# First attention: another order of the projections, scores and transposes on TensorE

## What is computed

```python
x = x + jnp.tanh(g_xattn[0]) * _L0_xattn_ref(ctx_768, _layernorm(x, axis=-1), mask_BxS2_bk0, ...)
x = x + jnp.tanh(g_ffn[0]) * _L0_ffn_ref(_layernorm(x, axis=-1), ...)
...
x = x + jnp.tanh(g_xattn[3]) * _L3_xattn_ref(_layernorm(x, axis=-1), ctx_768, ...)
x = x + jnp.tanh(g_ffn[3]) * _L3_ffn_ref(_layernorm(x, axis=-1), ...)
```

## Time and profile before

| what | us |
|---|---|
| median of the three runs | 1800.82 |
| lowest, highest | 1793.05, 1805.83 |
| the profiled execution's own time | 1798.77 |
| its span, first to last instruction | 1796.9 |

### The profile page before, as it was taken

One profiled execution on the slowest core, in us unless ns is written; L12 is line 12 of the kernel. 1 busy time (PEld: TensorE's weight loads), 2 busy tenths in 40 slices (PEclk: granted clock), 3 DMA queues, 4 the chain that ended last, 5 costly groups with the idle time before them and its releaser, 6 DMA issues.

```text
span 1796.9 us, 31011 instructions
## 1 busy us (share of the span) xinstructions
PE 1619.2 (90%) x9150; PEld 1153.7 (64%) x9150; DVE 981.3 (55%) x3200; ACT 624.8 (35%) x1772; POOL 333.5 (19%) x465
## 2 busy tenths in 40 slices
PE   6898899859999999999999999799998998887787
PEld 2555555659999866666666667567776446665555
DVE  4778787542222244444444435645555666884764
ACT  3555555412323233333333333133332004552232
POOL 4555555320000130000000000100000122333000
PEclk8999999869999989999999989899998999998887
DMA  4000005248999610000000000100000001310000
GB/s 109 15 18 20 20 19 146 65 138 298 321 327 319 232 41 13 7 12 12 12 12 6 1 4 16 31 26 19 19 25 1 27 25 35 91 56 1 1 19 19
DMA packets 86297, 115.80 MB, mean 64 GB/s; under 512 B 16610, under 2 KB 77762, under 8 KB 81090
## 3 DMA queue, kind: packets, MB, share of 16 engines
q1 hardware_dynamic: 82722, 110.43, 19.1%
q0 software_dynamic: 2432, 4.34, 0.8%
q10 hardware_dynamic: 1056, 0.01, 0.0%
HBM read 104.51 MB, written 6.95 MB: 62 GB/s over the span
## 4 chain that ended last, share of the span: by engine, by line
PE 73%; issue 9%; DVE 7%; ACT 4%; DMA 2%; POOL 2%; ACTq 1%; SPq 0%; DVEq 0%; POOLq 0%
PE bank L2293 14%; PE bank L2406 8%; PE bank L2589 7%; PE bank L2379 5%; PE bank L2682 5%; PE bank L2352 5%; PE bank L2390 4%; PE bank L2436 4%; PE bank L2603 3%; PE bank L2344 3%; PE bank L2635 3%; PE bank L2651 3%; PE bank L2754 2%; DMA work<-in_F_b1c 2%; DVE work L1542 1%
## 5 line engine op out<-in xcount | busy, mean ns | idle before, releaser
L1052 ACT ACTIVATE work<-bank,work 100x361 f32<-100x361 f32 (+1 forms) x272 | 158.9, 591 | 253.5 <-DVE work L1542 231.6
L1551 DVE COPY work<-bank 128x300 f32<-128x300 f32 (+1 forms) x272 | 123.2, 490 | 175.6 <-PE bank L2390 174.9
L2406 PEld LDWEIGHTS bank<-work 128*100 128x100 f32 x1760 | 185.4, 171 | 45.5 <-issue 31.4
L2406 PE MATMUL bank<-work 128*100 128x64 f32 (+1 forms) x1760 | 188.2, 258 | 4.2 <-DVE work L1551 4.2
L2589 PE MATMUL bank<-work 128*128 128x128 f32 x1216 | 144.4, 277 | 3.7 <-DMA work<-in_F_b1c 3.7
L1905 DVE SCALAR_TENSOR_TENSOR work<-bank,work 128x128 f32<-128x128 f32 x160 | 56.1, 351 | 163.8 <-PE bank L2589 151.6
L2589 PEld LDWEIGHTS bank<-work 128*128 128x128 f32 x1216 | 142.0, 193 | 5.3 <-issue 3.5
L1542 DVE TENSOR_REDUCE work<-bank 100x1 f32<-100x361 f32 x208 | 101.8, 528 | 70.9 <-PE bank L2379 65.7
L823 POOL TENSOR_TENSOR work<-work,neg_half 100x1 f32<-100x1 f32 x96 | 52.5, 547 | 391.8 <-DVE work L1498 390.1
L2379 PE MATMUL bank<-work 64*100 64x361 f32 (+1 forms) x512 | 119.0, 542 | 1.1 <-ACT work L1037 0.6
L2293 PE MATMUL bank<-L_WkvT,work 96*128 96x512 f32 x192 | 98.2, 637 | 15.8 <-ACT work L1013 14.9
(11 more groups left out here) (306 smaller groups left out, 2907.9 us busy)
## 6 DMA issues: line engine op xcount, KB each, us to landing
work<-in_F_w SPq DMA_DIRECT2D x58, 1024.0 KB, 5.5
work<-in_ctxT SPq DMA_DIRECT2D x64, 135.4 KB, 2.1
work<-in_ctx SPq DMA_DIRECT2D x32, 192.0 KB, 2.5
work<-in_F_b SPq DMA_DIRECT2D x20, 128.0 KB, 5.8
work<-sorted_x SPq DMA_DIRECT2D x20, 128.0 KB, 2.5
sorted_y<-work SPq DMA_DIRECT2D x20, 128.0 KB, 5.3
work<-in_ctx SPq DMA_DIRECT2D x32, 78.8 KB, 2.4
F_weight<-in_F_w SPq DMA_DIRECT2D x2, 1024.0 KB
```

Source lines behind the costliest of these rows:

```text
L1052: nc.scalar.activation(pr[:, 0:NK], S_bank[k][0:T, 0:NK], ACT.Exp, bias=nmax[k][0:T, :], accum_out=rsum[j][0:T, h:h + 1]).then_inc(s.exped ...
L1551: nc.vector.tensor_copy(PT[k][:, 0:CH, :], PT_bank[k][:, 0:CH * T].rearrange("p (c t) -> p c t", c=CH)).then_inc(s.probs_copied.sem, 1)
L2406: ins = nc.tensor.matmul(to, PT[k][:, c, :], values, start=(c == 0), stop=(c == CH - 1))
```

## The change

In the first attention PE turns the context of batch t + 2 (steps 0 and 1) ahead of the first scores; turns x (step 2) ahead of the probabilities' turn; puts steps 6 and 8 ahead of the scores of heads 2 and 3; and steps 3 and 4 ahead of the first weighing, with 9 and 10 behind it. On ACT step 8's copy moves ahead of the exponentials of heads 2 and 3, since its program reads the same tables.

```diff
--- before.py
+++ after.py
@@ -30,9 +30,9 @@
 
 
 PAIRS = (2, 4, 2, 0)
-EARLY = ((0, 1, 5), (0, 1, 2), (0, 1, 2), (0, 1, 2))
+EARLY = ((0, 1, 5, 2), (0, 1, 2), (0, 1, 2), (0, 1, 2))
 GROUPS = (
-    ((2, 6, 8, 3), (4, 9, 10, 7)),
+    ((6, 8, 3, 4), (9, 10, 7)),
     ((3, 4), (5, 6), (7,), (8,)),
     ((3, 4), (5, 6)),
     ((3, 4),),
@@ -2519,27 +2519,28 @@
                 def first_attend(t, q):
                     j = q % 2
                     started = not (isinstance(t, int) and t == 0)
+                    ahead(t, q, EARLY[0][:2])
                     scores(t, j, 0)
                     scores(t, j, 1)
-                    ahead(t, q, EARLY[0][:2])
                     if started:
                         o_turn(t - 1, 1 - j, (q + 2) % RING)
                     ahead(t, q, EARLY[0][2:])
-                    for p in range(PAIRS[0]):
-                        probs_turn(t, j, 2 * p)
-                        probs_turn(t, j, 2 * p + 1)
-                        if p == 0:
-                            if started:
-                                project(t - 1, 1 - j)
-                            scores(t, j, 2)
-                            scores(t, j, 3)
-                            ahead(t, q, GROUPS[0][0])
-                        else:
-                            ahead(t, q, GROUPS[0][1][3:])
-                        weigh(t, q, 2 * p)
-                        weigh(t, q, 2 * p + 1)
-                        if p == 0:
-                            ahead(t, q, GROUPS[0][1][:3])
+                    probs_turn(t, j, 0)
+                    probs_turn(t, j, 1)
+                    if started:
+                        project(t - 1, 1 - j)
+                    ahead(t, q, GROUPS[0][0][:2])
+                    scores(t, j, 2)
+                    scores(t, j, 3)
+                    ahead(t, q, GROUPS[0][0][2:])
+                    weigh(t, q, 0)
+                    weigh(t, q, 1)
+                    ahead(t, q, GROUPS[0][1][:2])
+                    probs_turn(t, j, 2)
+                    probs_turn(t, j, 3)
+                    ahead(t, q, GROUPS[0][1][2:])
+                    weigh(t, q, 2)
+                    weigh(t, q, 3)
 
                 if L == 0:
                     for n in ALONE:
```

## The result

| | before | after |
|---|---|---|
| median of 8 runs, us | 1800.23 | 1815.95 |
| lowest to highest | 1793.05 to 1805.83 | 1809.5 to 1822.64 |
| ratio, 95% interval | | 1.0095 (1.0073 to 1.0116) |
| profiled execution | 1798.77 | 1815.89 |

The ratio is that of the changed kernel's time to the time of the kernel before. The changed kernel is 16 us slower by the medians (0.87%), 0.95% by the ratio, whose interval lies above 1. The forecast was 1838 in a range of 1799 to 1860: the direction was right, the loss that was forecast more than twice the measured one.

The account below looks back on a forecast made before the run. The prediction took a closed ring through PE and DVE's fixed chain behind the later scores to bound the changed stage. 1798.77 + 5 (full clock) + 33 (lower clock) gave 1837, stated as 1838 us, range 1799 to 1860.

Parts of the forecast that it names:

- The three waits: PE's waits in each turn for ACT's copies, at steps 5, 3 and 10: all close, 26.4 us together.
- the third gap: PE's wait at step 10 for ACT's copy of step 4, 8.7 us over 14 turns: gone.
- The wait for the exponentials: PE, after the first scores start later and delay maxima and exponentials: 0.15 us of wait left.
- The ring: Later scores, DVE's chain, last weighing, next later scores: turn 21.6 us against 20.77, PE idle 2.6 us before the last weighing.
- The sum at full clock: First attention's turns without any fall of the clock: +5 us in total.
- the three light turns: Turns 0, 1 and 13, with little residual and router work or no next norm: -3 us together.
- The clock: Long PE gaps before the last weighing bring half clock, nine of eleven at 3.7 us each: +33 us.
- Rival A: Ring binds before the last weighing but the clock stays up or rarely falls: 1804 us, no measurable change; chance 0.25.
- Rival B: DVE keeps up and PE's waits in the first attention simply vanish: 1772 us; chance 0.09, whole or in part.

Follow-up runs that it names:

- part_step4: Kernel before with only step 4 moved ahead of the first weighing, ACT's order as before: 1802.12 us, ratio 1.0026.
- step4_act: Kernel before with step 4 ahead of the first weighing and ACT's copy of step 8 ahead of the later exponentials: 1788.72 us, ratio 0.9945.
- part_scores: Kernel before with only the later scores moved behind steps 2, 6 and 8, ACT in the changed kernel's order: 1819.33 us, ratio 1.0109.
- dve_ahead: Changed kernel with 2.0 us of DVE's work moved from behind the later maxima to ahead of them: 1783.4 us, ratio 0.9909 to the kernel before.
- mid2: Changed kernel with two unused matmuls ahead of the last weighing, only in turns 2 to 12: 1810.57 us, ratio 1.0078 to the kernel before.
- again: The changed kernel run once more, unaltered: 1816.49 us, ratio 1.01 to the kernel before.
- early_act: The whole change except that the later scores stay where the kernel before had them, ahead of steps 6 and 8: 1785.94 us, ratio 0.9932.
- part_turns: Kernel before with only steps 0 and 1 ahead of the first scores and step 2 ahead of the probabilities' turn: 1795.76 us, ratio 0.9983.
- fill2: Changed kernel with two unused matmuls on PE ahead of the last weighing: 1809.66 us, ratio 1.0077 to the kernel before.
- split_act: Later scores early, first weighing between steps 8 and 3, later probabilities' turns split among the steps, ACT's step 8 copy early: 1780.11 us, ratio 0.991 to the kernel before.
- fill4: Changed kernel with four unused matmuls on PE ahead of the last weighing: 1820.85 us, ratio 1.0132 to the kernel before.
- early_scores: Kernel before with steps 0, 1, 2 and 4 moved as in the change, later scores and ACT's order as before: 1800.75 us, ratio 1.0008.
- all_closed: Later scores early, first weighing between steps 8 and 3, later probabilities' turn between 4 and 9, ACT's old order: 1791.91 us, ratio 0.9958 to the kernel before.
- mid1: Changed kernel with one unused matmul ahead of the last weighing, only in turns 2 to 12: 1811.1 us, ratio 1.0083 to the kernel before.

## Why the prediction was wrong in size and right in kind

- **The three waits close.** As forecast; none of them is in the list any more. But the term's condition was incomplete: step 4 ahead of the first weighing pays only since ACT copies step 8 early. The prediction named that move as part of the change and gave it no price; part_step4 against step4_act (21.10 against 20.01 us a turn) shows that it carries the third gap.
- **The wait for the exponentials.** 0.15 us taken, 0.23 measured (290.46).
- **The ring.** Forecast 10.6 + 11.0 = 21.6 us and a gap of 2.6; measured 10.64 + 10.76 = 21.40 and 2.31. The chain on DVE is 8.88 instead of 9.13. part_scores and dve_ahead show it from both sides.
- **The sum at full clock.** +5 forecast. mid2 has 251.9 against 246.6 us in the turns of the table without t = 8: +5.3, with one stretch of 3.4 us at half clock still in it (t = 1 and 2, which it shares with the changed kernel) and none in t = 3 to 7 and 9 to 12. The forecast's +5 has t = 8 and the light turns 13 and 14 in it as well. There the changed kernel won 1.8 us (t = 13, 18.90 against 20.68 from last weighing to last weighing, clock 1.00) and 0.6 (t = 14), and t = 0 won 1.0; t = 1 lost 0.2. So the three light turns won 2.5 of the 3 forecast, the full ones lost 0.63 us each instead of 0.85 (21.40 against 20.77), and t = 2 lost 0.9, not the 0.1 to 0.2 forecast for it.
- **The clock: the step that failed.** "I take nine of eleven gaps: 9 x 3.7 = 33 us." That gaps of this size bring the half clock was right: eight stretches came, with twelve gaps. Wrong was the length of one. I took the mean of five stretches of the old trace, 7.3 us; here they are 3.4 (five) and 6.8 us (three), 4.7 on average. And the price was a little less than half of the length: the turns of the changed kernel without t = 8 sum to 264.5 us against mid2's 251.9, so 12.6 us. Of the 37.5 us at half clock 3.4 lie in t = 8 and 3.4 are shared with mid2, so 12.6 us stand for 30.7: 0.41 us for each, where I had taken a half. again has 10.2 us for 23.7, 0.43. Why the stretches are shorter than the old ones stays open. Other waits inside them are no answer: of the old ones, those of 13.5 and 6.6 us have idle time in them (busy 11.96 and 5.84), but that of 10.1 us has none, nor have the 10 us of mid2 behind the loop's return. The old trace also has a fifth gap of this size from the full clock, in the stage itself, which the prediction left out: 2.17 us before 365.66, with 30.7 us at half clock from 365.07 on. In the two executions of the changed kernel a stretch that began while PE stood in its gap lasted 6.8 us, and one that began behind the gap 3.4; the old ones do not follow this, since that of 6.6 us began 0.6 us behind its gap.
- **Where the measured time lies.** The two profiled executions differ by 17.2 us in span. Turns 0 to 12 have 17.9 of it without t = 8, and t = 8 has 0.8. From the start of turn 13 to the first matmul of the mixture it is 3.5: turn 15 alone is 4.8 us longer at half clock, which the prediction did not have. The rest of the kernel has 0.8, and the part before turn 0 is 5.9 us shorter. That last part is 3.2 us longer in the second execution of the changed kernel, so it can't be put down to the change; in that execution the same terms are 15.5, 0.5, 2.2, 1.5 and -2.7, 17.0 in all. That the forecast's terms with the clock as measured, 5 + 13 = 18, come near the 16 us of the medians is in part luck, since these other terms nearly cancel.
- **Rival A** (the clock stays up) is excluded by the 0.50 rows, and its time, 1804, lies 12 us below. Its price for the ring was right. **Rival B**, 1772, is excluded: DVE did not keep up. What it would have asked for is what dve_ahead does, and the gain then comes. The rule of the Trainium skill named there (Perfetto Trace Analysis, Identifying the Most-Contended Engine) speaks for PE by occupancy; the section adds that TensorE's headroom is to be judged by its use in FLOPs (MFU) or by the busy share of its weight loads. By occupancy PE has 18.86 of 21.40 us and DVE 16.57; by the weight loads, 11.98 us, DVE would be ahead. The time of the changed kernel was set by neither alone, but by the ring through both. The advice of the Trainium skill in Optimization Strategy of the same page, to find what blocks and make that come sooner, fits dve_ahead.

## What to carry to other kernels

In this kernel a matmul that starts a long chain on another engine belongs as early as it can go, however small it is, and projections that fill time belong behind it. Before an order is changed, follow the ring through the other engine's fixed order, from the moved instruction to where its result is waited for: an engine that is 77% busy (16.57 of 21.40 us) was part of the bound here. Three short waits of PE and one long one of the same sum did not have the same price: 26.4 us of waits of 0.6 to 0.9 us had no stretch at half clock, 25.9 us in waits of 1.4 to 2.5 had eight.

## What was not expected of the hardware

- Four stray matmuls of 96 x 512 took 3.43 us, 0.86 each; the scores of two heads (64 rows, 512 columns each) take 1.04 us together, start to start. Two matmuls on the two halves of the rows seem to run in part beside each other; this was not tested apart.
- The loop's return costs 2.1 us over a normal turn before, and up to 9.4 in the variants (t = 8 in the table less the turns beside it). The wait for the exponentials there, 1.1 to 2.7 us in the kernels that have it, does not order them (part_step4 has the shortest, 1.07, and pays 5.1); the length at half clock in t = 8 does. Without any the return costs 2.1 to 2.6 us (before, step4_act, early_act), with 3.4 us 3.5 and 4.1 (part_turns, fill2), with 6.8 us 5.1 to 6.2 (part_step4, split_act, fill4, dve_ahead), with 10.2 us 6.7 to 7.5 (early_scores, all_closed, mid2), with 12.6 and 14.9 us 8.7 and 9.4 (mid1, part_scores). The changed kernel has no such wait: the 3.5 us at half clock in its t = 8 are the end of a stretch that began in t = 7, and the turn costs 2.2. In split_act and dve_ahead, the fastest, the return still costs 3 to 4 us more than with the clock up.
